# Gated cross-attention with routed experts on one core: the residual sum accumulated by TensorE and copied by ScalarE

## The reference, cut

```python
q = rope(proj(layernorm(x), Wq, bq)); k = rope(proj(ctx, Wk, bk)); v = proj(ctx, Wv, bv)
p = softmax(where(mask == 0, -1e9, q @ k.T / sqrt(8)))          # 16 heads of 8
x = x + tanh(g_xattn) * ((p @ v) @ Wo.T + bo)                   # the sum that is moved here
logits = layernorm(x) @ Wr + br                                 # 8 experts, the best one is taken
y = gelu(layernorm(x) @ W1[e] + b1[e]) @ W2[e] + b2[e]
x = x + tanh(g_ffn) * y * softmax(logits)[e]
```

## Time and profile before

| | us |
|---|---|
| median of 3 runs | 287.91 |
| lowest and highest | 287.01, 290.49 |
| the profiled execution's own time | 287.01 |
| its span | 285.2 |
| TensorE busy in the span | 229.3 (80%) |
| VectorE busy | 189.1 (66%) |
| GpSimd busy | 180.3 (63%) |
| ScalarE busy | 164.9 (58%) |

### The profile page before, as it was taken

How to read it: one execution, slowest core, us unless ns; L and a number is a source line. 1 busy time by engine, 2 the same in 40 slices (tenths; PEclk the granted TensorE clock), 3 DMA queues, 4 the chain that set the end, 5 groups by cost and what they waited for, 6 DMA issues and landing times.

```text
span 285.2 us, 11006 instructions
## 1 busy us (share of the span) xinstructions
PE 229.3 (80%) x3785; PEld 193.4 (68%) x3785; DVE 189.1 (66%) x639; ACT 164.9 (58%) x482; POOL 180.3 (63%) x222
## 2 busy tenths in 40 slices
PE   1357888987988987789879896598789899999950
PEld 1245677765866765667768675376689799999950
DVE  4546778788798888988867868886575344444310
ACT  1236669696677886568865886436464344444410
POOL 5366757568467889467896686704877654555550
PEclk9999999999799999979996999979999999999995
DMA  7801466546543673314351221333143443110100
GB/s 216 230 15 28 102 148 169 143 103 144 144 129 79 171 177 67 105 32 126 67 150 37 42 48 34 76 85 86 45 143 91 123 119 79 50 33 24 39 21 0
DMA packets 58537, 26.53 MB, mean 93 GB/s; under 512 B 38608, under 2 KB 53989, under 8 KB 58484
## 3 DMA queue, kind: packets, MB, share of 16 engines
q1 hardware_dynamic: 55204, 20.02, 29.3%
q0 software_dynamic: 2272, 4.46, 4.7%
q10 hardware_dynamic: 1008, 1.35, 1.6%
HBM read 16.57 MB, written 5.51 MB: 77 GB/s over the span
## 4 chain that ended last, share of the span: by engine, by line
PE 43%; DVE 19%; issue 11%; ACT 10%; POOL 5%; DMA 5%; SPq 3%; DVEq 0%; POOLq 0%
PE ps L752 13%; DVE mx L1240 5%; PE ps L771 4%; PE ps L795 4%; PE ps L770 3%; PE ps L733 3%; PE ps L735 3%; PE ps L734 3%; ACT vx L644 2%; DVE qk L1185 2%; SPq L411 2%; ACT kT L630 2%; DMA w_r<-in_W_last_row 2%; ACT qk L616 2%; DMA kbd<-kT 2%
## 5 line engine op out<-in xcount | busy, mean ns | idle before, releaser
L565 POOL DMA_INDIRECT out<-fin,got x39 | 37.9, 971 | 28.2 <-DVE fin L1299 23.4
L1240 DVE TENSOR_REDUCE mx<-ps 128x16 f16<-128x1024 f32 x32 | 39.0, 1219 | 12.8 <-PE ps L813 12.7
L752 PE MATMUL ps<-w_f,hT 128*128 x312 | 44.6, 286 | 0.1
L517 POOL DMA_INDIRECT rows<-x_all,dest_i x32 | 33.3, 1041 | 17.0 <-DVE x_all L1075 9.5
L795 PE MATMUL ps<-vx,pr 128*64 128x32 f32 x1024 | 38.0, 229 | 4.9 <-DVE on L1175 4.0
L795 PEld LDWEIGHTS ps<-vx,pr 128*64 128x64 f32 x1024 | 34.5, 144 | 8.9 <-issue 5.3
L544 POOL TENSOR_TENSOR rot<-qk,cf 128x256 f32<-128x256 f32 x32 | 23.4, 732 | 24.7 <-ACT qk L616 17.6
L752 PEld LDWEIGHTS ps<-w_f,hT 128*128 128x128 f32 x312 | 37.8, 191 | 1.1 <-issue 0.3
L1299 DVE SCALAR_TENSOR_TENSOR fin<-ps,got 128x128 f32<-128x128 f32 x39 | 13.7, 351 | 35.9 <-PE ps L752 35.9
L531 POOL TENSOR_TENSOR stk<-rot,stk 128x256 f16<-128x256 f32 x32 | 21.5, 671 | 20.4 <-DVE stk L1253 20.4
L594 ACT ACTIVATE pr<-ps 128x1024 f32<-128x1024 f32 x32 | 32.7, 1021 | 2.2 <-PE ps L843 1.6
(11 more groups left out here) (158 smaller groups left out, 585.1 us busy)
## 6 DMA issues: line engine op xcount, KB each, us to landing
kbd<-kT SPq DMA_DIRECT2D x128, 32.0 KB, 2.5
got<-rows SPq DMA_DIRECT2D x39, 72.0 KB, 2.0
w_f<-in_W_rows SPq DMA_DIRECT2D x8, 256.0 KB, 2.9
w_r<-in_W_last_row SPq DMA_DIRECT2D x8, 256.0 KB, 3.2
w_f<-in_L_ffn_W SPq DMA_DIRECT2D x8, 256.0 KB, 4.7
x_all<-in_x SPq DMA_DIRECT2D x3, 512.0 KB, 5.2
xt_all<-in_x_t SPq DMA_DIRECT2D x3, 512.0 KB, 4.8
ct_all<-in_ctx SPq DMA_DIRECT2D x3, 512.0 KB, 4.5
```

Source lines behind the costliest of these rows:

```text
L517: pool.indirect_dma_start(out=rows, out_offset=bass.IndirectOffsetOnAxis(ap=dest_i[:, t:t + 1], axis=0), in_=x_all[:, t, :], in_offset=Non ...
L565: pool.indirect_dma_start(out=out_d, out_offset=bass.IndirectOffsetOnAxis(ap=got_i[:, u % GOT, R_ID:R_ID + 1], axis=0), in_=fin[:, u % FRI ...
L752: mm = pe.matmul(o, hT[:, par, c, :], w2_f[:, bass.ds(e, 1), c, :].rearrange("p o n -> p (o n)"), start=False, stop=(c == FC - 1))
L1240: dve.tensor_reduce(mx[:, t % 2, :].rearrange("p (w h) -> p w h", w=2)[:, :, 0:8], ps_s[:, :].rearrange("p (w h k) -> p w h k", w=2, k=S), ...
```

## The change

The sum of x and the attention output is no longer made by VectorE. TensorE starts the accumulation in `ps_op` with a product of the transposed x (`xt_all`, already loaded for the projection) and `id_wr`, which holds the identity and, in its last 8 columns, the centred router weights; the bias rows and `onT` times `wo_x` are accumulated on it. ScalarE copies the 136 columns into `x_all` at the top of its step, ahead of the exp. VectorE's add goes, and so do the 8 further columns of the projection and ScalarE's copy of them. TensorE's projection now waits for VectorE's read of q where it waited for the logits copy. The statistics on VectorE wait for `x2_done` as before, which ScalarE now gives; the placing of a group's rows has an explicit wait for it.

```diff
-        wqx = sb("wqx", [P, QX])
+        wqx = sb("wqx", [P, D])
...
-        ps_lx = bank[6][:, D:QX]
-        ps_qx = bank[6][:, 0:QX]
...
             def step(i):
+                t = i - 6
+                if live(t):
+                    act.wait_ge(op_done, t + 1)
+                    act.activation(x_all[:, t, 0:QX], ps_op, ACT.Copy).then_inc(x2_done, 1)
                 t = i - 4
                 if live(t):
                     act.wait_ge(st_done, t + 1)
...
                     act.wait_ge(qe_ev, t + 1)
-                    act.activation(x_all[:, t, R_LOGIT:R_LOGIT + NE], ps_lx, ACT.Copy).then_inc(lx_ev, 1)
...
-                        pe.wait_ge(s_wc, 3)
+                        pe.wait_ge(s_wc, 2)
...
-                    wait(pe, lx_ev, t)
-                    pe.matmul(ps_qx, xt_all[:, t, :], wqx[:, :], start=True, stop=True)
+                    wait(pe, qe_ev, t)
+                    pe.matmul(ps_q, xt_all[:, t, :], wqx[:, :], start=True, stop=True)
...
                     pe.wait_ge(onT_ev, t + 1)
-                    pe.matmul(ps_op, pick, c_h[:, :], start=True, stop=False)
+                    pe.matmul(ps_op, xt_all[:, t, :], id_wr[:, :], start=True, stop=False)
+                    pe.matmul(ps_op, pick, c_h[:, :], start=False, stop=False)
                     pe.matmul(ps_op, onT[:, t % 2, :], wo_x[:, :], start=False, stop=True).then_inc(op_done, 1)
...
-            dve.tensor_tensor(wqx[:, D:QX], wr_n[:, :], bank[0][:, D:QX], ALU.subtract).then_inc(s_wc, 1)
...
-                t = i - 6
-                if live(t):
-                    dve.wait_ge(op_done, t + 1)
-                    dve.wait_ge(lx_ev, t + 1)
-                    dve.tensor_tensor(x_all[:, t, 0:QX], ps_op, x_all[:, t, 0:QX], ALU.add).then_inc(x2_done, 1)
                 if third is not None:
+                    dve.wait_ge(x2_done, min(T, i - 5))
                     route_place(third)
```

More of the change, by code:

```diff
@@ L264, in build @@
         kbd_ld = [sem(f"kbd_loaded{i}") for i in range(RING)]
-        (bn_s, bn_a, rv1, rs1, qkv_done, qe_ev, lx_ev, k_ev, v_ev, rope1, rope2, rope_done, hi_done, lo_done, mrow,
+        (bn_s, bn_a, rv1, rs1, qkv_done, qe_ev, k_ev, v_ev, rope1, rope2, rope_done, hi_done, lo_done, mrow,
          stk_done, kT_ev, qT_ev, s_done, mx_done, mxT_done, mxT_ev, st_done, p_rdy, pv_done, rden_done,
          on_done, onT_done, onT_ev, op_done, x2_done, bn2_s, bn2_a) = (sem(n) for n in (
-             "stats", "mean_var", "var_eps", "rstd_made", "projected", "q_scaled", "router_part_copied", "k_copied", "v_copied",
+             "stats", "mean_var", "var_eps", "rstd_made", "projected", "q_scaled", "k_copied", "v_copied",
              "rope_cos", "rope_sin", "rope_made", "hi_made", "lo_made", "mask_row_made", "stacks_transposed",
```

## The result

| | median us | lowest and highest | ratio to before |
|---|---|---|---|
| before (5 runs) | 287.01 | 284.08, 290.49 | 1 |
| changed (5 runs) | 294.95 | 293.20, 307.23 | 1.0266, interval 1.0199 to 1.0333 |

The kernel became slower, by 2.7%; forecast were 297.0 us, which is 3.2% over the 287.91 known then. The ratio rests on the changed kernel's three executions of 293.20 to 294.95 us (mean granted clock 0.975 to 0.988) and not on the two longer ones (0.948 and 0.942), and as every profile of it is of such a longer one (spans of 302.6 to 305.4 us), the profile of `e7_after_filled`, the same kernel but for a few unread products, stands in for the usual ones.

The account below looks back on a forecast made before the run. A ring of waits, no full engine, bounds the attention stage. Even intervals +10.9, long -1.9, next step's table work -1.0, stage end +1.7: +9.7 us, 296.7 like the profiled run, said as 297.0; range 289.5 to 303.

Parts of the forecast that it names:

- The ring: Attention stage: ScalarE's copy waits for the output product, holding up exp, `mxT`, L785 and `kT`; 5.45 us a step.
- strict floor: Attention stage: all links are waits or one engine's order, so no interval can be shorter than 5.45 us.
- The even intervals: Seventeen even `kT` intervals of the attention stage go to 5.45 us each, 92.65 against 81.72: +10.9 us.
- The long intervals: Ten long `kT` intervals of the attention stage stay ruled by what rules them; -1.0, -2.0 and +1.1, together -1.9 us.
- +1.1 of half-clock products: Long intervals: the added product at half clock in two of the four runs, 2 x 0.56 us.
- -1.0 for VectorE's adds: Long intervals, run 102.72 to 127.01: the chain passes VectorE's removed add four times, saving 1.0 us.
- The end of the attention part: After the last `kT`: +1.7 us for late exp and sum, -1.0 where VectorE's table work sets the next step.
- exp comes 1.3 late and nothing covers it: Stage end: exp of 189.20 about 1.3 us late, x2 0.4 more, then GpSimd's scatters uncovered: +1.7 us.
- The signs named beforehand: Copy waits 32 times some 0.85 us, L785 released by `mxT`, even intervals 5.3 to 5.6, VectorE 9 us less busy.
- The long steps pay for the short ones: Rival, attention stage: ring of 5.25, even intervals +7.5, ten long ones absorb 0.5 each; +3.3, 291.2 us; chance 0.20.
- VectorE sets the pace: Rival, attention stage: VectorE's queue rules every step, each loses 0.30 us, 9.6 in all; 278.3 us; chance 0.04.
- The clock falls: Rival, attention stage: half of 26 steps at half clock, 1.0 us each, 13 us more; 310 us; chance 0.14.

Follow-up runs that it names:

- e7_after_filled: Changed kernel with the last tile's projection products made twice more, unread, in TensorE's steps 32 and 33; profiled span 293.2 us, two of four runs 299.6 and 301.4.
- e1_copy_late: Changed kernel with ScalarE's copy of the sum moved from the top of its step to behind k's mask row, ahead of `kT`; 289.6 to 298.3 us, no ratio.
- e9_mxT_first: Changed kernel with `mxT` put ahead of exp on ScalarE, both still behind the copy of the sum; four runs of 285.1 to 296.2 us.
- e6_no_add: Kernel before without VectorE's add and nothing in its place, attention output left out of the sum; 287.11 against 288.91 us, ratio 0.9990.
- e0_again: The changed kernel run again as it is, for another profile and time; median 296.11 against 288.80 us of the kernel before, ratio 1.0255.
- e4_product_early: Changed kernel with x's product and the bias product ahead of the wait for `onT`, transposed `on` in another bank; 287.6 to 293.2 us.
- e11_vector_early: Changed kernel with x's and bias products ahead of the wait for `onT`, and the sum copied by VectorE; 288.53 against 289.25 us before, ratio 0.9936.

## Why the prediction was right, step by step

*The ring*, the step on which all hung, held link by link: 0.18, 0.90, 0.54, 0.65, 2.03 and 1.21 measured against 0.20, 0.92, 0.53, 0.64, 1.98 and 1.17, so 5.51 against 5.45. `e1_copy_late` and `e9_mxT_first` show that the links are the right ones. It is no strict floor, as the prediction said it was: three of the 27 intervals took 5.39 (`e7_after_filled`). The added product is 0.33 of it, against 0.28 on the chain in the earlier trace rows. ScalarE went on 0.18 after the copy's start, 0.10 before its row ended, and 0.90 after the start of exp, 0.12 before that row of 1.02 ended: about the same overlap for a short and a long row. The Trainium skill (Perfetto Trace Analysis, Optimizing Scalar/DVE Operations) says of the data-access overhead of each instruction, not of its whole duration, that it shows in a profile at about twice the time that it holds the engine, since the acknowledgement of the write overlaps the next instruction. The trace agrees in that the overlap hardly grows with the row.

*The even intervals* cost 93.63 - 81.72 = +11.9 (in `e7_after_filled`), forecast +10.9: the 0.06 of the ring. In the three profiles of the changed kernel itself they cost 12.0 to 13.1.

*The long intervals* gave back more than forecast, 57.53 - 60.84 = -3.3 against -1.9. Which parts: the half-clock stretches of before (0.86 and 0.81) did not come again in the attention stage, whose granted clock was 1.00, so the +1.1 of half-clock products never fell due and five intervals of 5.9 to 6.5 sank to the ring's length or near it; that the clock alone did this isn't shown. The -1.0 for VectorE's adds is not borne out by `e6_no_add`. And one interval grew by 1.0 us, the 23rd, from 5.42 to 6.42, which I had not seen coming. In `e0_again` TensorE's products that place a group's rows (L687) stand there ahead of the product of x and waited 0.89 us for VectorE's `oh`, and ScalarE's copy waited 1.20 with them. The sum of the two terms, +9.0 forecast and +8.6 measured, is closer than its parts, which is luck.

*The end of the attention part* was forecast at +0.7. At full clock it took 17.42 against 17.87, -0.5, though with the filling; at 0.50 it took 8.7 us more. So the step "exp comes 1.3 late and nothing covers it" has no full-clock profile of its own and isn't shown. The range had a slip: from 293.5 to 303 it takes the 2 us of the long intervals off below but does not add them above, where they give 305.

*The signs named beforehand* came as said (the copy's waits 0.8 us, 25 times in the stage), except that VectorE was 5.8 us less busy instead of 9.

*The rivals.* "The long steps pay for the short ones" came nearer than its chance of 0.20 says. In the changed kernel they paid 3.3 of 11.9. But the rival spoke of a ring of 5.25, and `e4_product_early` has just that: the even intervals cost 7.5 there and the long ones gave back 4.65, near the rival's +7.5 and -5.0. My objection, that two long intervals in a row can't both use the same slack, isn't borne out there: the first two, 6.13 and 5.92, fell to 5.40 and 5.27. How much of that is the clock's, 1.00 in that stage against 0.95 before, isn't separated. What the rival had wrong is the ring, which was 5.51. "VectorE sets the pace" is out by `e6_no_add`. The advice of the Trainium skill (Perfetto Trace Analysis, Optimizing Scalar/DVE Operations) to offload to ScalarE has a saturated VectorE as its condition; here VectorE was busy in 114.4 of 138.0 us of the stage, and its relief bought nothing that could be measured. "The clock falls" did occur, in every profile of the changed kernel, but not where I put it: the attention stage kept 1.00, and the clock fell at its end. Its price of 1.0 us a step was right: at half clock the step took 6.57 against 5.51 (rows below).

## What to carry to other kernels

Before work is moved to an engine with idle time, write out that engine's order and ask what stands behind the moved instruction's wait, and who reads that: here 0.28 us of copying held up exp and `mxT` by 1.2 us, and only `mxT`'s reader made it cost. Then compare the new ring with the mean step of before, 5.28 us: at 5.18 (no product) the 27 intervals grew by 0.9 us, at 5.25 (early product) by 2.9, at 5.51 by 8.6. The idle time that looks free (25 us ahead of `k`) can be used only at its own place in the order, as the late copy did. And relief of an engine is worth what the chain says of it, not what its busy share says: 9.3 us of VectorE's work bought nothing that could be measured.

## What the runs showed of the hardware

The granted clock at the end of the attention part was 0.50 or 0.51 on average in the three profiles of the changed kernel and 1.00 in that of the filled one, while the stage ahead of it ran at 1.00 in all four. In `e0_again` the clock fell from 2.4 to 1.2 GHz near 189 us and stayed there until about 216.5. Ahead of the fall TensorE had been busy 0.90 of 2 us (first row: 187 to 189 us) and had paused 1.60 us ahead of L786:

```profile
187.00:189.00 2.00, 0.90 (x6) 0.65 (x6) 1.75 (x8) 1.07 (x3) 1.22 (x3) 1.00 0.24 37
189.00:191.00 2.00, 1.40 (x17) 1.23 (x18) 1.78 (x8) 0.69 (x3) 1.62 (x2) 0.57 0.23 59
191.00:193.00 2.00, 2.00 (x45) 1.77 (x43) 0.00 (x0) 0.74 (x2) 1.47 (x2) 0.50 0.29 74
```

At 1.2 GHz the ring of the change turns more slowly still. Copy to copy on ScalarE, same profile:

```profile
195.87 0.28 ACT L591 ACTIVATE x_all<-ps 128x136 f32<-128x136 f32 x1 [2.11 <-PE ps L859]
...
202.44 0.28 ACT L591 ACTIVATE x_all<-ps 128x136 f32<-128x136 f32 x1 [2.11 <-PE ps L859]
```

That is 6.57 us against 5.51, with ScalarE waiting 2.11 for the output product. In the kernel before the clock dips near the same place too, to an average of 0.90 over its 17.87 us, and comes back sooner (0.53 from 186 to 188 us, 1.00 again from 190). Why it stays down so much longer in the changed kernel's profiles is open. The ring of the change can't be the whole reason, since `e11_vector_early`, where exp follows `onT` at once, ran the same stretch at 0.61, with TensorE busy in 19.89 of its 19.96 us.
